# Layer 0 of a three-layer interaction kernel from four product tiles and a tile of squares, with the last adds over d on GpSimd

## What is computed

```python
xk = x0 = e                                   # [b, 32, 16]
for W in (W0, W1, W2):
    xk = relu(einsum('bmd,bhd,mhk->bkd', x0, xk, W))
    outs.append(sum(xk, axis=2))              # sum over d
h = concatenate([*outs, dense_ctx], axis=1)   # 192 + 16 values
h = maximum(h @ W_top1 + b_top1, 0)           # 208 x 512
h = maximum(h @ W_top2 + b_top2, 0)           # 512 x 256
y = h @ W_top3                                # 256 x 1
```

## Time and profile before

| | before |
|---|---|
| median of 3 runs (lowest, highest) | 647.42 us (647.08, 648.91) |
| span of the profiled execution | 646.9 us |
| TensorE busy | 587.2 us (91%) |
| VectorE busy | 584.8 us (90%) |
| GpSimd busy | 470.5 us (73%) |
| ScalarE busy | 358.1 us (55%) |
| data moved by DMA | 96.5 MB, mean 149 GB/s |
| mean granted TensorE clock | 0.997 of full speed |

### The profile page before, as it was taken

The page is one execution under the profiler, slowest core; times in us unless marked ns, Lnnn a source line. Parts: engine busy times, 40 slices in busy tenths (PEclk is TensorE's granted clock), DMA queues, the critical chain, the costliest instruction groups (busy, mean ns, idle before and its releaser), DMA issues.

```text
span 646.9 us, 7779 instructions
## 1 busy us (share of the span) xinstructions
PE 587.2 (91%) x2896; PEld 209.9 (32%) x2896; DVE 584.8 (90%) x329; ACT 358.1 (55%) x594; POOL 470.5 (73%) x405
## 2 busy tenths in 40 slices
PE   0078898999898989999999999999999999999998
PEld 0023332333232323333334323333334323333455
DVE  1039897999999999999999999999999999999994
ACT  0006472756646564757656575747676465736552
POOL 6677769588888888898888888888989783803011
PEclk9999998999999999999999999999999999999999
DMA  5286585728073643737181735547380826300000
GB/s 161 50 313 165 208 285 147 279 39 304 22 232 131 183 179 73 290 64 296 31 313 22 221 140 146 216 81 281 54 308 4 275 85 199 162 3 2 1 2 1
DMA packets 27138, 96.51 MB, mean 149 GB/s; under 512 B 7414, under 2 KB 12540, under 8 KB 22876
## 3 DMA queue, kind: packets, MB, share of 16 engines
q1 hardware_dynamic: 18908, 93.90, 43.4%
q0 software_dynamic: 8192, 2.11, 2.9%
HBM read 80.25 MB, written 15.73 MB: 148 GB/s over the span
## 4 chain that ended last, share of the span: by engine, by line
DVE 42%; PE 24%; issue 12%; POOL 11%; DMA 8%; SPq 2%; ACT 1%; DVEq 0%; POOLq 0%; ACTq 0%
DVE prod L489 40%; PE acca L590 10%; POOL emb L362 7%; PE accb L590 5%; DMA rows<-field_dram 4%; PE acc L560 3%; POOL prod L380 3%; PE spread L633 2%; DMA field_dram<-zb_field 2%; DMA emb<-in_table,idx 1%; SPq L280 1%; PE accb L611 1%; PE acc L611 1%; DVE prod L470 1%; ACT zb_field L720 1%
## 5 line engine op out<-in xcount | busy, mean ns | idle before, releaser
L362 POOL DMA_INDIRECT emb<-in_table,idx x256 | 247.9, 968 | 81.7 <-issue 67.3
L590 PE MATMUL acca<-prod,w 128*64 128x512 f32 x1024 | 230.4, 597 | 3.5 <-DVE prod L489 2.4
L590 PE MATMUL accb<-prod,w 128*64 128x512 f32 x960 | 216.4, 596 | 13.3 <-DVE prod L489 13.3
L380 POOL TENSOR_TENSOR prod<-rows,mates 128x1024 f32<-128x1024 f32 x70 | 164.3, 2381 | 13.1 <-issue 12.6
L489 DVE TENSOR_TENSOR prod<-rows,x1a 128x2048 f32<-128x2048 f32 x64 | 146.2, 2287 | 6.0 <-PE acca L590 3.0
L489 DVE TENSOR_TENSOR prod<-rows,x1b 128x2048 f32<-128x2048 f32 (+1 forms) x65 | 146.4, 2254 | 4.4 <-PE acca L590 3.7
L489 DVE TENSOR_TENSOR prod<-rows,x2a 128x2048 f32<-128x2048 f32 x64 | 146.3, 2287 | 1.1 <-PE accb L590 0.8
L489 DVE TENSOR_TENSOR prod<-rows,x2b 128x2048 f32<-128x2048 f32 x64 | 146.3, 2287 | 0.0
L590 PEld LDWEIGHTS acca<-prod,w 128*64 128x64 f32 x1024 | 72.0, 138 | 147.2 <-issue 136.3
L590 PEld LDWEIGHTS accb<-prod,w 128*64 128x64 f32 x960 | 65.6, 137 | 155.8 <-issue 113.8
L725 ACT ACTIVATE x1a<-acc 64x512 f32<-64x512 f32 x62 | 35.3, 570 | 128.1 <-PE acc L560 127.4
(11 more groups left out here) (74 smaller groups left out, 258.6 us busy)
## 6 DMA issues: line engine op xcount, KB each, us to landing
rows<-field_dram SPq DMA_DIRECT2D x30, 2048.0 KB, 13.7
field_dram<-zb_field SPq DMA_DIRECT2D x32, 256.0 KB
mates<-field_dram SPq DMA_DIRECT2D x16, 512.0 KB, 3.8
emb<-in_table,idx POOLq DMA_INDIRECT x256
field_dram<-zb_field SPq DMA_DIRECT2D x32, 128.0 KB
field_dram<-zb_field SPq DMA_DIRECT2D x16, 192.0 KB
rows<-field_dram SPq DMA_DIRECT2D x2, 1024.0 KB, 7.3
rows<-field_dram SPq DMA_DIRECT2D x1, 1536.0 KB, 12.8
```

The costliest lines, as they stand in the source:

```text
L362: pool.indirect_dma_start(out=emb[q % EMBS][:, j * EMB:(j + 1) * EMB], out_offset=None, in_=table, in_offset=bass.IndirectOffsetOnAxis(ap= ...
L380: nc.gpsimd.tensor_tensor(prod0[:, (q * L0 + k) % RING0, :], rows[:, slot(q, t), :], mates[:, :], ALU.mult).then_inc(s_prod0p, 1)
L590: mm = nc.tensor.matmul(acc[j % 2][side * HID:(side + 1) * HID, :], (w1 if layer == 1 else w2)[:, step, :], prod[:, (made(layer, s, half, ...
```

## The change

1. **Layer 0 from four tiles and the squares.** `LAYER0_TILES` is now (1, 2, 3): products of fields that stand 1, 2 and 3 apart in the list. A fourth product tile multiplies `mates` by a new tile `across`, read from the list with distance 4, 8, 12 and 16 in its four blocks of 32 rows. The 32 squares come from a new tile `squares` (64 x 512: the two halves of the 32 fields one above the other), which ScalarE squares in place, and which TensorE contracts over 32 rows each with two matmuls. So a period has four products in place of five, and five contractions as before.
2. **Two more transfers per period** on SyncE's queue: `across` (512 KB) behind `mates`, and `squares` (128 KB) ahead of `rows`; the latter waits until layer 0 of the period before is summed.
3. **The last add over d** is a fourth GpSimd instruction; VectorE's 24 reduces for `za` and `zc` are gone. The last one of all (`zb`) stays.
4. **`halve12(0)` stands behind** the six gathers for period 3.
5. The order of the first transfers is tile 1, tiles 2 and 3, `squares`, tile 0, tiles 4 to 7. `prod0` has four buffers. `h2` lies in `h1`. 

```diff
-LAYER0_TILES = (0, 1, 2, 3, 4)
-MATES = 104
+LAYER0_TILES = (1, 2, 3)
+MATES, FIELDS_LISTED = 104, 32
...
-    L0 = len(LAYER0_TILES)
-    RING0 = 5
+    L0 = len(LAYER0_TILES) + 1
+    RING0 = 4
+    BLOCKS = P // FIELDS
...
-    FIRST = [(0, 2), (2, 2), (4, 1), (5, 3)]
+    FIRST = [(1, 1), (2, 2), (0, 1), (4, 4)]
...
+    SQUARES = L0
...
-        SUM0[2 * q - 2, 1] = [(k, q) for k in range(3, L0)]
+        SUM0[2 * q - 2, 1] = [(SQUARES, q), (L0 - 1, q)]
...
                 sp.dma_start(mates[:, :], part).then_inc(s_mates, 16)
+                at = (q % LISTS * LENGTH + MATES) * N
+                part = bass.AP(field_dram.tensor, at + 4 * N, [[4 * N, BLOCKS], [N, FIELDS], [1, N]])
+                sp.dma_start(across[:, :], part).then_inc(s_across, 16)
+
+            def fields_in(q):
+
+                wait_for(sp, s_l0, q * (L0 + 1))
+                at = (q % LISTS * LENGTH + MATES) * N
+                part = bass.AP(field_dram.tensor, at, [[HALF, 2], [N, FIELDS], [1, HALF]])
+                sp.dma_start(squares[:, :], part).then_inc(s_fields_in, 16)
...
             for g, (t, count) in enumerate(FIRST):
+                if t == 0:
+                    fields_in(0)
                 spread_rows(0, t, count, s_first[g])
             for q in range(1, PERIODS):
                 list_fields(q)
                 mates_in(q)
+                fields_in(q)
...
+                other = across[:, :] if k == 0 else rows[:, slot(q, LAYER0_TILES[k - 1]), :]
+                nc.gpsimd.tensor_tensor(prod0[:, k, :], other, mates[:, :], ALU.mult).then_inc(s_prod0p, 1)
...
-                nc.gpsimd.tensor_tensor(by_d[:, :, 0:PAIR], by_d[:, :, 0:PAIR], by_d[:, :, PAIR:QUAD], ALU.add).then_inc(done, 1)
+                nc.gpsimd.tensor_tensor(by_d[:, :, 0:PAIR], by_d[:, :, 0:PAIR], by_d[:, :, PAIR:QUAD], ALU.add).then_inc(s_pair, 1)
+                pool.wait_ge(s_pair, n)
+                nc.gpsimd.tensor_tensor(to, by_d[:, :, 0], by_d[:, :, 1], ALU.add).then_inc(done, 1)
...
             gather_early(3)
-            halve12(0)
             gather(3, 10, 2)
             gather(3, 3 * STRETCH, STRETCH)
 
+            halve12(0)
...
             for j in range(SUBS):
-                for i, unit in enumerate(vector_units(j)):
+                for unit in vector_units(j):
                     outer(*unit)
-                    if j % 2 == 1:
-                        if i == 2 and j > 1:
-                            sum12(j // 2 - 1)
-                        if i == 5 and j == SUBS - 1:
-                            sum12(LAST)
-                        if i == 6 and j > 1 and (j % 4 == 1 or j == SUBS - 1):
-                            sum3(j // 2 - 1)
...
             def layer0(k, q):
+                if k == SQUARES:
+                    pe.wait_ge(s_squares, q + 1)
+                    for c in range(2):
+                        part = slice(c * FIELDS, (c + 1) * FIELDS)
+                        mm = nc.tensor.matmul(acc0[c * HID:(c + 1) * HID, :], w0[part, SQUARES, :], squares[part, :],
+                                              start=False, stop=False)
+                    mm.then_inc(s_l0, 1)
+                    return
...
+            def square_fields(q):
+                act.wait_ge(s_fields_in, (q + 1) * 16)
+                nc.scalar.activation(squares[:, :], squares[:, :], ACT.Square).then_inc(s_squares, 1)
```

More of the change, by code:

```diff
@@ L186, in cin_tower_kernel @@
         mates = sb("mates", [P, N])
+        across = sb("across", [P, N])
+        squares = sb("squares", [2 * FIELDS, HALF])
         prod0 = sb("prod0", [P, RING0, N])
@@ L464, in product0 @@
             def product0(q, k):
[L465 removed]
                 if k == 0:
                     dve.wait_ge(s_mates, (q + 1) * 16)
[L468 to L471 removed]
+                    dve.wait_ge(s_across, (q + 1) * 16)
+                elif q == 0:
+                    rows_wait(q, LAYER0_TILES[k - 1])
+                elif k == 1:
+                    rows_wait(q, 0)
+                if q > 0:
+                    dve.wait_ge(s_l0, summed_before(q - 1, k) + 1)
+                other = across[:, :] if k == 0 else rows[:, slot(q, LAYER0_TILES[k - 1]), :]
+                nc.vector.tensor_tensor(prod0[:, k, :], other, mates[:, :], ALU.mult).then_inc(s_prod0v, 1)
             def outer(layer, s, half, u):
@@ L676, in _ @@
             pe.wait_ge(s_w0sum, 1)
-            for k in range(L0):
+            for k in ORDER0:
                 layer0(k, 0)
@@ L823, in _ @@
             input2(0, 1)
+            square_fields(1)
             input1(2, 0)
@@ L886 @@
     w0 = np.asarray(given.pop("L0_rec_W0"))
-    given["w0"], given["w0_swapped"] = np.zeros((2, 128, len(LAYER0_TILES), w0.shape[2]), w0.dtype)
+    given["w0"], given["w0_swapped"] = np.zeros((2, 128, len(LAYER0_TILES) + 2, w0.shape[2]), w0.dtype)
     seen = set()
-    for k, tile in enumerate(LAYER0_TILES):
+    for k in range(len(LAYER0_TILES) + 1):
         for q in range(128):
-            a, b = field_of(q + MATES), m[q, tile]
+            a, b = field_of(q + MATES), across_of(q) if k == 0 else m[q, LAYER0_TILES[k - 1]]
             if (a, b) not in seen:
@@ L896 @@
                 seen |= {(a, b), (b, a)}
+    for q in range(2 * FIELDS_LISTED):
+        a = field_of(MATES + q % FIELDS_LISTED)
+        assert (a, a) not in seen or q >= FIELDS_LISTED
+        given["w0"][q, len(LAYER0_TILES) + 1] = w0[a, a]
+        seen.add((a, a))
     assert len(seen) == w0.shape[0] * w0.shape[1]
```

95 lines of the change are left out of this document (43 added, 52 removed).

## The result

The changed kernel takes **687.86 us**; the kernel before, run beside it, 648.01. The ratio is 1.0613, with a 95% interval of 1.0593 to 1.0634. The span of the profiled execution is 686.0 us, against 646.9: 39.1 us more. The prediction was 654.2 us with a range of 640 to 664. The sign was right, the time lies 23.9 us above the range, and rival 4's 675 comes nearest.

The account below looks back on a forecast made before the run. No engine bounds the whole: transfers before 118.7 us, mostly VectorE to 568, then TensorE. Start +9.7, reduces -3.8, late fifth product -0.8, squares' shape +1.7: +6.8 on 646.9 is 653.7, median 654.2 us; range 640 to 664.

Parts of the forecast that it names:

- rival 4: Late rows every period: gathers behind GpSimd's second product miss the turn, 1 us and more in 13 periods, 675; chance 0.06.
- the cases: The two transfers: given out by blocks to 4 and 2 engines (8.1 us more), or spread over 16 (2.6 us).
- The reduces: VectorE from 118.7 to 568 us: 19 reduces gone at 0.20 us each, -3.8 us.
- the late fifth product: GpSimd with four products is in time, so the 0.8 us stall on VectorE goes: -0.8 us.
- the squares' shape: TensorE's squares' pair on 32 rows: 0.36 us for going over and back, +1.7 us in all.
- The gathers' gain: Six gathers ahead of the adds: TensorE's 2.42 us wait at 101.49 and slow first unit go, -3.7 us there.
- the price of a packet: Narrow transfers: 0.17 us per 4 KB packet, 8.1 us more on two engines; at most 0.25 us and 12.8 us.
- The sign I named for it: Profile after: across takes 8 us and more from issue to landing, with most of the 16 engines idle meanwhile.
- +5.1, +9.8, +9.7: Start: delays in us of periods 0, 1 and 2 against the kernel before; only +9.7 entered the sum.
- the steady part: From period 3 on: rows landed long before their use, and 8 us more still fit.
- rival 2: TensorE's squares' matmuls run one behind the other and change shape, 1.2 us a period: 651 with spread transfers; chance 0.05.
- Rival 1: Both transfers spread over all engines (2.6 us): VectorE 3.1 us sooner than 118.69, sum -6.0, 641.4; chance 0.24.

Follow-up runs that it names:

- the doses: Changed kernel with squares in two transfers and across in one with 4, 8 or 16 rows outermost: 671.93, 656.53 and 646.85 us.
- the run with the new order: Changed kernel with both transfers spread, rows of tiles 1 to 3 first behind mates, and the product of across last: 644.69 us, ratio 0.9955 against the kernel before.
- the first experiment: Changed kernel with across read by four transfers of 32 rows and squares by two: 646.73 us, ratio 0.9979 against the kernel before.

## Why the prediction was wrong

**What held.** The decision between the cases did: transfers with 4 and 2 outermost rows behave as if 4 and 2 engines carried them, and the loss is these two transfers (41.1 us of it go when they are spread, which leaves the change at 0.998 of before). The reduces were put at -3.8 and the late fifth product at -0.8, with +1.4 of the squares' shape against them, and B to C shrank by 4.0 wherever landing left it alone. In the earlier trace rows the wait of TensorE for GpSimd at 185.99 is that fifth product. GpSimd's new add takes 0.29 to 0.30 us for 64 columns, the upper bound, 24 x 0.30 = 7 us, and lies beside other work as said. The gathers' gain was put at 3.7; where nothing swallows it, it is 4.3 in a pair of profiles and 3.5 in the medians.

**The step that failed first: the price of a packet.** "Its lower price, because few engines draw at a time" was 0.17 us for 4 KB. It is 0.26 to 0.32 by the doses, and above the 0.25 of the list that I held for the dear end. Between 4 outermost and four transfers of 32, the first landing moved by 49.27 - 41.45 = 7.8 us for 24 packets, 0.33 each. 32 packets on an engine are then 8 to 11 us for `across` where 5.4 stood in the sum; from its issue to VectorE's first product it was 50.01 - 34.97 = 15.0 us, with `mates` ahead of it and other transfers beside it. My price came from packets of other sizes, at a time when all 16 engines worked, and the reason I gave for scaling it down was no row at all. The sign I named for it, that most engines would be idle, can't be read from the share: that stays full at 1.09, and each packet takes longer.

**The second: the start adds up.** I let each period's delay be swallowed in part by the next (+5.1, +9.8, +9.7, each counted against the kernel before). Measured it is +11.4 at period 0's first product of sub-period 0 (61.06 - 49.71), +23.4 at the end of period 1's layer 0 and +32.2 at B, so 11.4, 12.0 and 8.8 per period. Period 1's `mates` come only after period 1 is turned, behind period 0's layer 0, and each period pays its own narrow transfers. For period 1 I had that chain and only its price was low; for period 2 I had 17.1 us from `mates` to landed rows, and it is 134.61 - 112.88 = 21.7 (GpSimd's second product started at 134.61, and `mates` was issued at 112.88), and nothing behind it hides that. The 22.5 us between +9.7 and +32.2 can be laid out along my own chain. The landed rows of the three periods missed their place by 54.03 - 48.1 = 5.9 us, by 24.65 - 17.1 = 7.6 (95.46 - 70.81 from `mates` on) and by 21.7 - 17.1 = 4.6: 18.1 us are the price of the packets, three times over. Another 2.7 lie between the landed rows of period 1 and `mates` of period 2 (112.88 - 95.46 = 17.4, against 14.7), a term that the sum lacked: TensorE at 0.50 of its clock, where eight records took 3.68 us and the squares' four 1.60. The last 1.7 are small pieces. ScalarE's squares were taken as hidden from period 2 on, which they were; in the start TensorE waited 1.27 us for them in the run with the new order.

**The third: the steady part.** "From period 3 on, rows landed long before their use, and 8 us more still fit." The table says that 6 us more already cost 2.2, and the 11 that came cost 10.9. The sign that I named for this, waits of more than 1 us behind 200 us, is there six times. Rival 4 had this mechanism with its place and order (rows not there for GpSimd's second product, gathers behind it, the turn late) and 1 us per turn, against a measured mean of 9.7 / 6 = 1.6 in six turns of the twelve between B and C, and got 0.06 because its condition was put at 12.8 us. With 6.9 lost in place of the -3.2 or so of the sum (-3.8 - 0.8, and what of the squares' +1.7 lies ahead of mark C), this step missed by 10 us and the start by 22.5; together they are the 32.3 us between 653.7 and 686.0. The last 1.4 us to the median are no mechanism: I put it 0.5 us above the span, and in each execution on record the time is 1.8 to 1.9 us above it.

**The squares' shape** was priced at 0.36 us, and costs 0.30. In the kernel before, the second unit of a sub-period and the one behind its two pairs of layer 0 start at

```profile
252.38 3.60 PE L590 MATMUL acca<-prod,w 128*64 128x512 f32 x16
...
257.53 7.04 PE L590 MATMUL acca<-prod,w 128*64 128x512 f32 x32
```

that is 5.15 us apart, and in the rows above, where the first pair is the squares', 254.50 - 249.05 = 5.45. The Trainium skill ("TensorEngine Tiling (Array Packing)", Tiling Modes) says that a change of the mode drains the engine; the trace has room for 0.30 us for going over and back, and no more. This term was sized rightly, and rival 2 with its 1.2 us is ruled out.

**Rival 1** (spread, 641.4) was in fact measured, as the first experiment: 646.7. It missed the start: B was to come 3.1 us sooner than before and came 1.8 later. With the new order B came at 118.96, so the order is 1.5 us of the 4.9. The traces place the rest in the closing of layer 0 of period 1: later data, the wait for ScalarE's squares, and the squares' pair itself. Rival 1 had put the last two at 0.6 us together, and they are 2.2 there. That the later data are the weight of 640 KB more, in a stretch where the queue's share is full, was argued and not tried alone.

## What to carry over

Count the outermost dimension of every new DMA: by the doses of 4, 8 and 16 here a transfer behaves as if it were spread over that many engines only, and it should be priced as packets on one of them, with the highest price per packet that the profile shows, not the lowest; splitting it into transfers with a wide outermost dimension costs some tenths of a microsecond of issue each (four took 1.82 us of SyncE's queue, one 0.67) and here gave back 41 us. When a transfer lands later, ask for every consumer how much slack it has, in the start (none, and it adds up over the periods) and in the steady part, and find the point from which it fails by the first engine that has other duties behind its wait. Work taken from a bound engine helps only if the one that gets it has room.

## What the runs showed of the hardware

- A busy DMA share says little: 1.09 with 216 GB/s against 1.01 with 389 in the same window of the same stage. A packet took 0.53 us on average there (6.7 KB) against 0.19 (4.6 KB), and 0.21 (5.3 KB) with both transfers spread.
- A packet of 4 KB cost 0.26 to 0.33 us of its engine when, by the outermost count, 4 to 16 engines carried a transfer of 128 packets and the rows of the other transfers ran beside it.
- Behind gaps TensorE's granted clock fell from 1.00 to 0.50 (1.2 GHz) in some profiles, and four records took 1.84 to 1.98 us in place of 1.07. It did so behind a gap of 3.41 us in one kernel and not behind one of 3.06 us in another with the same code up to there, and in the changed kernel behind one of 2.07 us and not behind one of 1.90, so the gap alone doesn't settle it.
- The same program can have the drop in one execution and not in the next: of 74 executions of the kernel before, 34 had a mean clock of 1.0 and the rest 0.997 or 0.995, at some 2 us more.
- Two matmuls on 32 rows between pairs on 128 rows cost 0.30 us more than a pair on 128 rows.
